# Weight preparation in another order: the output weight second, a third staging area, and the first sample's attention woven in anew

## The reference, cut to what matters

```python
z_l = jnp.einsum('bnd,ed->bne', h, W_lang)
z_g = jnp.einsum('bnd,ed->bne', h, W_grav)
v = jnp.einsum('bnd,ed->bne', h, W_V)
...                     # K from the products z_l z_l^T and z_g z_g^T
out = jnp.einsum('bnm,bmd->bnd', K, v)
return jnp.einsum('bnd,ed->bne', out, W_O)

x = _layernorm(x + _L0_gnn_ref(x, ...), axis=-1)      # attention over nodes
x = _layernorm(x + _L1_gnn_ref(x, adj, ...), axis=-1)
x = _layernorm(x + _L2_gnn_ref(x, adj, adj, ...), axis=-1)
x = _layernorm(x + _L3_gnn_ref(x, adj, ...), axis=-1)
```

## Time and profile before

| what | value |
|---|---|
| median of 3 runs | 2059.3 us (2059.19 to 2059.37) |
| profiled execution | 2057.45 us, of which the span 2055.6 us |
| TensorE busy | 2013.2 us, 98% of the span |
| weight loads of TensorE (PEld) | 1830.5 us, 89% |
| VectorE busy | 1645.6 us, 80% |
| ScalarE busy | 1061.9 us, 52% |
| mean granted TensorE clock | 0.995 of full |

### The profile page before, as it was taken

One profiled execution on the slowest core, in us unless ns is written; L12 is line 12 of the kernel. 1 busy time (PEld: TensorE's weight loads), 2 busy tenths in 40 slices (PEclk: granted clock), 3 DMA queues, 4 the chain that ended last, 5 costly groups with the idle time before them and its releaser, 6 DMA issues.

```text
span 2055.6 us, 34568 instructions
## 1 busy us (share of the span) xinstructions
PE 2013.2 (98%) x13436; PEld 1830.5 (89%) x13436; DVE 1645.6 (80%) x4398; ACT 1061.9 (52%) x1965; POOL 149.2 (7%) x198
## 2 busy tenths in 40 slices
PE   6899999999999999999999999999999999999997
PEld 6789899999999989999999998999999999999996
DVE  5577888888788888878888887888878888787885
ACT  5444546455454555546455554645545464554643
POOL 0000010000101000010100001000000100001010
PEclk9999999999999999999999999999999999999998
DMA  4100010000001000010000001001000100001000
GB/s 144 51 6 17 1 42 1 11 32 11 32 1 41 2 11 32 1 42 1 24 19 11 32 1 42 1 11 31 11 32 1 42 1 11 32 1 42 1 22 21
DMA packets 23652, 44.69 MB, mean 22 GB/s; under 512 B 2624, under 2 KB 2880, under 8 KB 23488
## 3 DMA queue, kind: packets, MB, share of 16 engines
q1 hardware_dynamic: 23488, 42.48, 6.0%
HBM read 25.70 MB, written 16.78 MB: 21 GB/s over the span
## 4 chain that ended last, share of the span: by engine, by line
PE 93%; DVE 3%; ACT 2%; issue 1%; DMA 0%; SPq 0%; POOL 0%; POOLq 0%; ACTq 0%; DVEq 0%
PE psum L499 12%; PE psum L484 12%; PE psum L334 11%; PE psum L473 8%; PE psum L474 7%; PE psum L342 7%; PE psum L424 6%; PE psum L530 6%; PE psum L338 5%; PE psum L524 4%; PE psum L525 4%; PE psum L428 3%; PE psum L511 3%; DVE vs L981 2%; PE psum L579 1%; PE psum L585 1%
## 5 line engine op out<-in xcount | busy, mean ns | idle before, releaser
L981 DVE TENSOR_TENSOR zs<-psum,zs 128x512 fp32r<-128x512 f32 (+1 forms) x456 | 265.9, 610 | 87.0 <-ACT zs L697 84.0
L697 ACT ACTIVATE zs<-psum 128x512 fp32r<-128x512 f32 (+1 forms) x456 | 233.4, 536 | 162.9 <-PE psum L484 106.3
L499 PE MATMUL psum<-xs,zs 128*128 128x256 f32 x2048 | 275.7, 285 | 0.0
L499 PEld LDWEIGHTS psum<-xs,zs 128*128 128x128 f32 x2048 | 258.0, 191 | 2.4
L697 ACT ACTIVATE vs<-psum 128x512 fp32r<-128x512 f32 x128 | 76.6, 599 | 301.4 <-PE psum L530 299.5
L342 PE MATMUL psum<-ident,full 128*128 128x128 f32 x1220 | 168.5, 275 | 15.9 <-DMA full<-in_L_gnn_wk_dram 5.0
L697 ACT ACTIVATE full<-psum 128x512 f32<-128x512 f32 x160 | 95.2, 595 | 154.0 <-PE psum L342 94.7
L342 PEld LDWEIGHTS psum<-ident,full 128*128 128x128 f32 x1220 | 139.3, 141 | 38.5 <-DVE full L1076 17.6
L424 PE MATMUL psum<-vs,zs 128*128 128x512 f32 x512 | 141.2, 397 | 1.6 <-ACT vs L697 1.6
L334 PE MATMUL psum<-vs,zs 128*128 128x512 f32 x512 | 140.7, 397 | 0.7 <-ACT zs L697 0.7
L1058 DVE BATCH_NORM_STATS2 stats<-full 128x6 f32<-128x512 f32 x192 | 129.9, 690 | 4.4
(11 more groups left out here) (192 smaller groups left out, 5195.4 us busy)
## 6 DMA issues: line engine op xcount, KB each, us to landing
full<-in_x_dram SPq DMA_DIRECT2D x32, 512.0 KB, 3.5
out_dram<-full SPq DMA_DIRECT2D x32, 512.0 KB, 2.9
full<-in_L_gnn_W_lang_dram SPq DMA_DIRECT2D x2, 1024.0 KB, 5.5
full<-in_L_gnn_W_grav_dram SPq DMA_DIRECT2D x2, 1024.0 KB, 8.2
full<-in_L_gnn_W_O_dram SPq DMA_DIRECT2D x2, 1024.0 KB, 5.8
full<-in_L_gnn_W_V_dram SPq DMA_DIRECT2D x2, 1024.0 KB, 5.5
full<-in_adj_dram SPq DMA_DIRECT2D x1, 256.0 KB, 2.6
bias_row<-in_L_gnn_bias_dram SPq DMA_DIRECT2D x1, 256.0 KB, 7.1
```

Of the source, the lines that this page charges most:

```text
L499: last = mm(halves(bank)[:, n, :], y[:, e, n * P:(n + 1) * P], HTH[s][:, e, :], start=(y is ZH[s][kind] and e == 0 and n == 0), stop=(y is ...
L697: return nc.scalar.activation(dst, src, func, **kw)
L981: return tt(dst, src, plain(hi), ALU.subtract)
```

## The change

The jobs run in the order l, o, g, vo for each layer, where they were l, g, o, vo. The parts get a third staging area, the home of layer 1's vo matrix (`w_hi[1]["vo"]`, `w_lo[1]["vo"]`), which is written only by the last job; parts v0 and g1 use it, and l1 and v1 use `XS[1]` and `VS[1]`. The waits follow. The mirror of an l job comes after the transposes of the o job, and so waits for that job's tiles to be emptied. On ScalarE and VectorE the second part is split before the first job is emptied, `prepare_adj` comes after the o job, the softmax of the first sample after the g job, and the split of part 3 between the two halves of attention.

```diff
-        jobs = [("l", 0), ("g", 0), ("o", 0), ("vo", 0), ("l", 1), ("g", 1), ("o", 1), ("vo", 1)]
+        jobs = [("l", 0), ("o", 0), ("g", 0), ("vo", 0), ("l", 1), ("o", 1), ("g", 1), ("vo", 1)]
...
-                 (w3l, nat_a, prep_pe, 12), (w3g, nat_b, w_split, 6), (w3o, nat_a, w_split, 8),
+                 (w3l, nat_a, prep_pe, 8), (w3g, nat_b, w_split, 6), (w3o, nat_a, w_split, 8),
...
-        load_of_job = {2: 2, 6: 6}
+        load_of_job = {1: 2, 5: 6}
...
         parts = [("l", 0), ("g", 1), ("v", 3), ("l", 4), ("g", 5), ("v", 7)]
-        part_hi = {"l": ZS[1][:, 0:4, :], "g": XS[1], "v": XS[1]}
-        part_lo = {"l": ZS[1][:, 4:8, :], "g": VS[1], "v": VS[1]}
-        part_free = (0, 0, 8, 16, 16, 24)
-        split_of_job = {0: 2, 1: 4, 3: 6, 4: 8, 5: 10, 7: 12}
+        stage_hi = (ZS[1][:, 0:4, :], XS[1], w_hi[1]["vo"])
+        stage_lo = (ZS[1][:, 4:8, :], VS[1], w_lo[1]["vo"])
+        part_stage = (0, 1, 2, 1, 2, 1)
...
+        part_free = (0, 0, 0, 12, 16, 20)
+        part_of_job = {0: 0, 2: 1, 3: 2, 4: 3, 6: 4, 7: 5}
...
-            sp.wait_ge(prep_pe, 28)
+            sp.wait_ge(prep_pe, 24)
             load(1, 0)
...
                     if kind == "vo":
-                        pe.wait_ge(prep_out, 4 * q)
-                    pe.wait_ge(w_split, split_of_job[q])
+                        pe.wait_ge(prep_out, 4 * (q - 1))
+                    pe.wait_ge(w_split, 2 * part_of_job[q] + 2)
...
-                        if t:
-                            pe.wait_ge(mirror_out, 3 * (q // 4 * 2 + min(q % 4, 2) - 1) + t)
+                        if t and q % 4 > 1:
+                            pe.wait_ge(mirror_out, 3 * (q // 4 * 2 + q % 4 - 2) + t)
...                                                     # mirror, on TensorE
-                    pe.wait_ge(prep_out, 4 * q + t + 1)
+                    pe.wait_ge(prep_out, 4 * (q if q % 4 else q + 1) + t + 1)
...                                                     # start, on TensorE
                 adj_x(0, 0)
+                prepare(1)
                 mirror(0)
-                prepare(1)
+                prepare(2)
                 k_rows(0, 0)
-                mirror(1)
-                prepare(2)
+                mirror(2)
                 prepare(3)
                 aggregate(0, 0, (0, 1, 2, 3))
                 prepare(4)
                 softmax_sums(0, 0)
+                prepare(5)
                 mirror(4)
-                prepare(5)
+                prepare(6)
                 sum_rows(0, 0)
-                mirror(5)
-                prepare(6)
+                mirror(6)
                 prepare(7)
...                                                     # start, on ScalarE
+                split_weight(1)
                 prepare(0)
-                split_weight(1)
                 split_adj_x(0, 0)
+                prepare(1)
                 mirror(0)
-                prepare(1)
+                split_weight(2)
+                prepare(2)
                 softmax_columns(0, 0)
-                split_weight(2)
-                mirror(1)
-                prepare(2)
                 softmax_rows(0, 0)
+                mirror(2)
                 attention_start(0, 0)
+                split_weight(3)
                 attention_end(0, 0)
                 prepare(3)
-                split_weight(3)
                 gates()
+                split_weight(4)
                 prepare(4)
-                split_weight(4)
+                prepare(5)
                 mirror(4)
-                prepare(5)
+                split_weight(5)
+                shift_x(0, 0)
+                prepare(6)
                 sum_row(0, 0)
-                shift_x(0, 0)
-                mirror(5)
-                split_weight(5)
-                prepare(6)
+                mirror(6)
...                                                     # start, on VectorE
                 split_x(0, 0)
-                prepare_adj()
+                split_weight(1)
                 prepare(0)
-                split_weight(1)
                 split_adj_x(0, 0)
                 prepare(1)
-                softmax_args(0, 0)
+                prepare_adj()
                 split_weight(2)
                 prepare(2)
+                softmax_args(0, 0)
...                                                     # after attention tiles 0 and 1:
+                    if not t:
+                        split_weight(3)
                 prepare(3)
-                split_weight(3)
                 prepare_gates()
+                split_weight(4)
                 prepare(4)
                 sum_squares(0, 0)
-                split_weight(4)
                 prepare(5)
-                scale_agg(0, 0)
                 split_weight(5)
                 prepare(6)
+                scale_agg(0, 0)
```

More of the change, by code:

```diff
@@ L245, in gnn_stack @@
         loads = [(w1l, nat_a, None, 0), (w1g, nat_b, None, 0), (w1o, nat_a, w_split, 2), (w1v, nat_b, w_split, 4),
-                 (w3l, nat_a, prep_pe, 12), (w3g, nat_b, w_split, 6), (w3o, nat_a, w_split, 8),
+                 (w3l, nat_a, prep_pe, 8), (w3g, nat_b, w_split, 6), (w3o, nat_a, w_split, 8),
                  (w3v, nat_b, w_split, 10)]
-        load_of_job = {2: 2, 6: 6}
+        load_of_job = {1: 2, 5: 6}
         parts = [("l", 0), ("g", 1), ("v", 3), ("l", 4), ("g", 5), ("v", 7)]
         part_nat = {"l": nat_a, "g": nat_b, "v": nat_b}
-        part_hi = {"l": ZS[1][:, 0:4, :], "g": XS[1], "v": XS[1]}
-        part_lo = {"l": ZS[1][:, 4:8, :], "g": VS[1], "v": VS[1]}
-        part_free = (0, 0, 8, 16, 16, 24)
-        split_of_job = {0: 2, 1: 4, 3: 6, 4: 8, 5: 10, 7: 12}
+        stage_hi = (ZS[1][:, 0:4, :], XS[1], w_hi[1]["vo"])
+        stage_lo = (ZS[1][:, 4:8, :], VS[1], w_lo[1]["vo"])
+        part_stage = (0, 1, 2, 1, 2, 1)
+        part_hi = [stage_hi[k] for k in part_stage]
+        part_lo = [stage_lo[k] for k in part_stage]
+        part_free = (0, 0, 0, 12, 16, 20)
+        part_of_job = {0: 0, 2: 1, 3: 2, 4: 3, 6: 4, 7: 5}
         hi_of = {(k, l): w_hi[l][k] for l in range(2) for k in names}
@@ L370, in prepare @@
                     if kind == "vo":
-                        a, c = (part_hi["v"], part_lo["v"]), (hi_of["o", l], lo_of["o", l])
+                        a, c = (part_hi[part_of_job[q]], part_lo[part_of_job[q]]), (hi_of["o", l], lo_of["o", l])
                         last = product(dst, [(a[0][:, e, cols], a[1][:, e, cols], c[0][:, e, :], c[1][:, e, :])
@@ L377, in prepare @@
                     else:
-                        hi, lo, rest = part_hi[kind], part_lo[kind], slice(t * P, U)
+                        hi, lo, rest = part_hi[part_of_job[q]], part_lo[part_of_job[q]], slice(t * P, U)
                         last = product(dst[:, rest], [(hi[:, e, cols], lo[:, e, cols], hi[:, e, rest], lo[:, e, rest])
@@ L706, in split_weight @@
                     part = slice(2 * h, 2 * h + 2)
-                    run(part_hi[kind][:, part, :], part_nat[kind][:, part, :]).then_inc(w_rounded, 1)
+                    run(part_hi[i][:, part, :], part_nat[kind][:, part, :]).then_inc(w_rounded, 1)
             def prepare(q, tiles=range(FT)):
@@ L720, in mirror @@
                 for t in range(1, FT):
-                    act.wait_ge(mirror_pe, 3 * (q // 4 * 2 + q % 4) + t)
+                    act.wait_ge(mirror_pe, 3 * (q // 4 * 2 + q % 4 // 2) + t)
                     run(hi_of[jobs[q]][:, t, 0:t * P], psum[1][:, t, 0:t * P]).then_inc(mirror_out, 1)
@@ L1040, in split_weight @@
                     part = slice(2 * h, 2 * h + 2)
-                    low(part_lo[kind][:, part, :], part_nat[kind][:, part, :],
-                        part_hi[kind][:, part, :]).then_inc(w_split, 1)
+                    low(part_lo[i][:, part, :], part_nat[kind][:, part, :],
+                        part_hi[i][:, part, :]).then_inc(w_split, 1)
             def norm_stats(s, j, layer, tiles=range(NT)):
```

## The result

The changed kernel takes 2045.19 us (median of 4 runs, 2044.50 to 2045.58) where the kernel before takes 2059.24 (4 runs, 2057.30 to 2059.37); the ratio is 0.9936, 95% interval [0.9922, 0.995]. The forecast was 2046.6 in a range of 2044.4 to 2050.2. The profiled execution took 2045.55 us against 2057.45 before, 11.9 less; the forecast for it was 12.7 less, 2044.75.

The account below looks back on a forecast made before the run. The loop was taken as TensorE's own, so only the start's 12.83 us of idle time and its clock effects could be won. Twelve steps summed to 77.43 against 90.13 us, 12.7 less: 2046.6 us, range 2044.4 to 2050.2.

Parts of the forecast that it names:

- the twelve steps: TensorE's start-to-start times from first weight product to the loop, forecast to sum to 77.43 us, 90.13 before.
- the new wait before the mirror of l0: Mirror of l0 waits until W_O's tiles are emptied: 3.25 us with 0.68 of flips, bounds 0.68 and 4.04.
- 64.46 + 0.60 + 2.48 + 0.39: Mirror of l1: W_O's first tile transposed, copied, VectorE's subtractions, then 0.39; put at 68.03, a step of 2.35 us.
- 0.98 + 0.39 - 0.45: Mirror of g1, 0.98 + 0.39 behind g1 with `sum_rows` 0.45 in between; forecast as 0.94 us.
- The attention came in time: Attention with the woven split of part 3 ends at 53.1, TensorE wants it at 55.0: 1.9 us of margin.
- part 4 was split early: Third area lets part 4 be split from about 56, once vo0 is through, not after l1.
- the rivals that stood on these: Attention late, 2049.1 us, chance 0.05; third area failing through late split or load, 2051.4 us, chance 0.03.
- the wait before g1: TensorE's 2.33 us gap before g of layer 1, with 2.44 of half clock behind it; forecast to go.
- a fall in one of the light stretches: Clock rival at 24.71 to 29.77 or 63.01 to 68.03: one fall costs 1.46 to 2.44 us; chance 0.22.
- the two examples of before: In the kernel before, the clock fell at 67.50 to 69.14 us but not at 33.50 to 41.10.
- The row that held at 1.00: Kernel before, 33.50 to 41.10 us: only transposes, TensorE busy 3.50 of 7.60, granted clock stayed 1.00.
- The rule that spoke against the change: Transposes not counting as activity, both new stretches would end at half clock: 2051.5 us; by the row 2046.6.

Follow-up runs that it names:

- e5: Changed kernel's new order of jobs without the third staging area, each split behind the job that frees its area; 2053.85 us.
- e1: The changed kernel run again unaltered, as the measure for the runs beside it; 2044.79 us.
- e4: Changed kernel with the split of part 3 put behind the whole attention on ScalarE and VectorE; 2045.27 us.
- e2: Changed kernel with six matmuls that nobody reads added on TensorE in the wait ahead of the mirror of l0; 2044.42 us.
- e3: Changed kernel with twelve transposes that nobody reads added on TensorE in the wait ahead of the mirror of l0; 2044.09 us.
- e6: Kernel before, old order of jobs, with the third staging area and splits of parts 4 and 5 moved ahead; 2049.14 us.
- e7: Changed kernel with tile 0 of g0, vo0, g1, vo1 ahead of the preceding mirror, parts 2 and 5 split before the mirror's copies; 2041.48 us.
- e10: e7 with k_rows' five transposes moved from behind g0 into the wait ahead of g0's tile 0; 2041.55 us, against 2042.51 for e7 repeated beside it.

## Why the prediction was right

*That the start is all that can be won* was right: the loop is the same within 0.4 us in all profiles.

*The waits.* Ten of the twelve steps came out within 0.1 us, the new wait before the mirror of l0 among them (forecast 3.25 with its flips, measured 30.08 - 26.91 = 3.17 at 0.113 a flip). Two steps hold small slips in their adding up: 64.46 + 0.60 + 2.48 + 0.39 gives 67.93, not 68.03, and 0.98 + 0.39 - 0.45 gives 0.92, not 0.94; both are lost in the sum. The attention came in time, part 4 was split early, and no load was late; the rivals that stood on these fell. One cause was put down wrongly: I let the third area remove the wait before g1, but e5 has none there with two areas. In the kernel before, part 4's area was free once vo0 was through, so that the place of its split, behind the emptying of l1, is what seems to have held it back; no run moves that split alone. The area's own work is part 2 and part 5, the v parts, which wait 2.51 us each without it.

*The clock* was the step that failed in the profiled execution. I gave a fall in one of the light stretches 0.22 at 1.46 to 2.44 us; it fell in the first one in all four profiles that have that stretch as it is (the changed kernel, e1, e4, e5), for 1.55 to 1.60, and not in the second one in any of the four. Where the stretch was filled, by e2, e3 and the five kernels with tile 0 first, the clock held. The start then came to 77.81 in e2 and 77.43 in e3; that the latter is the forecast's own sum is chance, as l0 alone was 0.17 longer than forecast. I had weighed the two examples of before as equals. Why the second stretch holds its clock stays open. The row that held at 1.00 was no safe ground: in e6 the same stretch of the old order did fall, and its twelve flips took 2.48 us in place of 1.50.

*The total* was 2045.19 against 2046.6. The forecast was taken from a median of 2059.3; beside the experiments the kernel before ran at 2057.39, 2056.73 and 2057.26. In e1 the difference is 12.6 us, against 12.7, with the fall of the clock (1.57) on one side and a shorter rest (83.14, where the profile of before had 84.38) on the other. Part of so close an agreement is luck: l0 (9.11 to 10.46 us over the profiles), the clock behind the mirror and the tail (83.14 to 84.38) each move by about 1 us or more, and the kernel before by itself ran from 2054.58 to 2060.36 us beside the experiments.

*The rule that spoke against the change.* The Trainium skill, "TensorE: Matmul & The Clock Gate", section "Part 4: PE-mode transpose", says that transposes do not count as activity for the clock gate. By the rule e3 should have fallen like e1; with twelve more transposes in the stretch it stayed at 1.00. This trace disagrees, and the measurement decides: in this stretch the clock fell where TensorE waited between transposes, not where it transposed with hardly a break. Waits between transposes are not enough by themselves, as the second stretch shows.

## What to carry to other kernels

A start that is written out by hand can be summed step by step from one profile: start-to-start times of TensorE's groups, and for each new wait the chain of the engine that ends it. Look for work that uses none of the banks or areas that are waited for (here tile 0) and put it ahead of the wait; in e7 it filled most of the wait and kept the clock. Look also at the chain behind: in e10 a filled wait came back at the next job. A reused staging area is a wait in disguise, and memory whose own use comes last can be lent until then.

## What the runs showed of the hardware that was not expected

TensorE held 1.00 of its clock through 4.98 us of nothing but transposes, busy 4.70 of the 5.40 us around them (e3), and lost it behind the same kind of instruction at 3.39 of 5.40 (e1). In the changed kernel it held the clock in the second light stretch, at 2.99 of 4.12. The first matmuls of a kernel are slow for a time that differs from run to run, and the granted clock does not show it: the first eight took 3.78 us in both kernels, against 1.98 for the same eight of l1, with the clock at 1.00 in the records from 12.1 to 16 us, and l0, the same 48 matmuls, took 9.11 to 10.46 us over the profiles with an unchanged beginning.
